# Splitting a bias on GpSimd instead of VectorE, and moving the statistics of the third batch ahead of the first sum of x1, in a one-core conv, MLP and mixture-of-experts block

## The reference

```python
h  = spiral_conv(ln(ln(x)) * gamma + beta)      # a complex decaying filter along the 1024 tokens
x1 = h + ln(x)
h  = ln(x1) * gamma + beta
x2 = x + silu(h @ w1 + b1) @ w2 + b2 + x1       # the dense layer; b2 is its second bias
out = x2 + experts(ln(x2))                      # 8 experts, the top two of each token
```

## Time and profile before

| | us |
|---|---|
| median of 3 runs (lowest, highest) | 457.8 (455.8, 460.84) |
| the profiled execution | 456.46 |
| its span, first to last instruction | 454.7 |
| PE busy | 374.8 |
| DVE busy | 345.9 |
| ACT busy | 320.1 |
| POOL busy | 274.8 |

### The profile page before, as it was taken

How to read it: one execution, slowest core, us unless ns; L and a number is a source line. 1 busy time by engine, 2 the same in 40 slices (tenths; PEclk the granted TensorE clock), 3 DMA queues, 4 the chain that set the end, 5 groups by cost and what they waited for, 6 DMA issues and landing times.

```text
span 454.7 us, 11189 instructions
## 1 busy us (share of the span) xinstructions
PE 374.8 (82%) x2716; PEld 322.2 (71%) x2716; DVE 345.9 (76%) x1310; ACT 320.1 (70%) x772; POOL 274.8 (60%) x339
## 2 busy tenths in 40 slices
PE   1273388797989797998994598999999999999970
PEld 1131257484858576776773498999999999999970
DVE  7999997978989988987628158777777777777770
ACT  5791586979797897977662565777777777777740
POOL 6990954575777798685747405775545454545451
PEclk9995599999989699999998579999999999999995
DMA  7649131020222222322212323454333333333200
GB/s 257 183 145 314 63 59 35 1 47 12 61 75 59 88 47 74 73 86 61 99 50 87 108 71 100 134 151 121 107 96 101 98 102 104 106 105 104 76 3 0
DMA packets 34434, 41.60 MB, mean 91 GB/s; under 512 B 5382, under 2 KB 29459, under 8 KB 34244
## 3 DMA queue, kind: packets, MB, share of 16 engines
q1 hardware_dynamic: 27236, 23.56, 18.1%
q0 software_dynamic: 7136, 17.33, 13.2%
HBM read 19.52 MB, written 18.92 MB: 85 GB/s over the span
## 4 chain that ended last, share of the span: by engine, by line
PE 59%; DVE 17%; issue 6%; POOL 5%; ACT 4%; POOLq 0%; DVEq 0%; ACTq 0%
PE up_p L998 12%; PE down_p L836 7%; PE up_p L825 7%; PE turn_p L998 6%; PE route_p L1017 6%; PE down_p L1017 6%; PE up_p L1017 6%; PE turn_p L813 5%; DVE stats L1097 3%; PE down_p L1007 2%; DVE work L1162 2%; DVE work L1160 2%; ACT work L648 2%; POOL sorted_rows L560 2%; PE route_p L874 2%
## 5 line engine op out<-in xcount | busy, mean ns | idle before, releaser
L597 POOL DMA_INDIRECT out<-result,out_id x91 | 89.2, 980 | 90.3 <-DVE result L1479 71.4
L560 POOL DMA_INDIRECT sorted_rows<-rows,pos x64 | 73.8, 1153 | 32.8 <-issue 16.8
L825 PE MATMUL up_p<-h_t,work 128*128 128x512 f32 x128 | 65.1, 638 | 10.4 <-ACT work L622 9.2
L836 PEld LDWEIGHTS down_p<-w_sb,work 128*128 128x128 f32 x512 | 60.6, 192 | 9.6 <-issue 9.6
L998 PE MATMUL up_p<-xt,work 128*128 128x128 f32 x488 | 66.5, 281 | 0.0
L787 ACT ACTIVATE work<-mw_c 128x256 f32 x182 | 65.6, 414 | 0.3 <-issue 0.2
L836 PE MATMUL down_p<-w_sb,work 128*128 128x128 f32 x512 | 63.0, 277 | 0.0
L998 PEld LDWEIGHTS up_p<-xt,work 128*128 128x128 f32 x488 | 61.0, 197 | 0.1
L772 ACT ACTIVATE hid_t<-up_p 128x512 f32<-128x512 f32 x61 | 36.4, 597 | 30.6 <-PE up_p L998 30.5
L813 PE MATMUL turn_p<-ident,work 128*128 128x128 f32 x192 | 29.7, 306 | 31.1 <-ACT work L648 11.5
L813 PEld LDWEIGHTS turn_p<-ident,work 128*128 128x128 f32 x192 | 25.2, 159 | 38.6 <-ACT work L648 11.6
(11 more groups left out here) (236 smaller groups left out, 810.2 us busy)
## 6 DMA issues: line engine op xcount, KB each, us to landing
tin<-sorted_rows SPq DMA_DIRECT2D x91, 136.0 KB, 2.1
resid<-in_x SPq DMA_DIRECT2D x8, 512.0 KB, 3.7
resid<-work POOLq DMA_DIRECT2D x8, 512.0 KB, 4.6
sorted_rows<-zeros SPq DMA_DIRECT2D x29, 136.0 KB, 2.2
out<-result,out_id POOLq DMA_INDIRECT x91
work<-in_mw SPq DMA_DIRECT2D x1, 1024.0 KB, 6.4
sorted_rows<-rows,pos POOLq DMA_INDIRECT x64, 2.5
work<-in_w SPq DMA_DIRECT2D x1, 256.0 KB
```

The lines of the kernel that those rows point to most:

```text
L560: g.indirect_dma_start(sorted_dram, bass.IndirectOffsetOnAxis(pos[b % 2][:, j:j + 1], 0), rows[b % ROWBUFS][:, j, :], None).then_inc(s_sor ...
L597: g.indirect_dma_start(out_rows, bass.IndirectOffsetOnAxis(out_id[k][:, :], 0), result[k][:, :], None, bounds_check=TOKENS - 1, oob_is_err ...
L825: t.matmul(dst, w1_g[:, k], half(h_t, h), start=True, stop=True).then_inc(s_up, 1)
L836: last = t.matmul(down_p[:, j * D:(j + 1) * D], silu[c % 2][:, j * TILE:(j + 1) * TILE], w2_sb[:, c, :], start=False, stop=c == FC - 1, sk ...
```

## The change

GpSimd now computes the remainder of the bias, in a new function `bias_halves` behind `sort_constants`, as three instructions, each awaited by the next; VectorE's two instructions for it are gone. And on VectorE the statistics and moments of x of batch 2 now stand ahead of `x1_sum(0)` and its statistics, where they stood behind them.

```diff
+            def bias_halves():
+                pool.wait_ge(s_whi, 1)
+                pool.wait_ge(s_ident, 1)
+                link(g.tensor_tensor(b2_lo, b2_rows, b2_hi[:, :].bitcast(f32), ALU.subtract))
+                link(g.tensor_scalar(b2_lo, b2_lo, ident[0:2, 1:2], None, ALU.mult))
+                g.tensor_tensor(b2_hi_lo[:, :], b2_lo, b2_first, ALU.add).then_inc(s_wsplit, 1)
...
             sort_constants()
+            bias_halves()
             x1_scales(0)
...
             def weights():
-                v.wait_ge(s_whi, 1)
-                link(d.tensor_tensor(b2_lo, b2_rows, b2_hi[:, :].bitcast(f32), ALU.subtract))
-                d.scalar_tensor_tensor(out=b2_hi_lo[:, :], in0=b2_lo, scalar=ident[0:2, 1:2], in1=b2_first,
-                                       op0=ALU.mult, op1=ALU.add).then_inc(s_wsplit, 1)
                 v.wait_ge(s_b1raw, 1)
...
             weights()
+            x_moments(2, x_statistics(2))
             x1_sum(0)
-            x_moments(2, x_statistics(2))
             rotated = rotate_re(1)
```

## The result

The changed kernel takes 464.9 us (median of 6 runs, 462.83 to 468.47), the kernel before 457.17 beside it (6 runs, 455.8 to 461.71). The ratio is 1.0154, 95% interval 1.009 to 1.0219: slower by about 7 us.

What follows compares the result with a forecast made beforehand. A prologue chain of waits through TensorE, VectorE, GpSimd and ScalarE was taken to bound the kernel. 0.2 + 3.5 + 2.0 - 0.1 = 5.6 us longer gave a forecast of 462.8 us, range 459.0 to 466.0.

Steps and rivals of the forecast that it cites:

- The lost cover: x1_scales(0) on GpSimd, no longer beside batch 2's one-operand statistics, waits on rotations and scans: 3.5 us longer.
- the four ends that the prediction names: x1_scales(0)'s instructions get through as rotate_re, rotate_im and two scans end: 46.3, 47.4, by 51.3 (power), 52.0.
- The bias: Three GpSimd instructions on 512 elements hold up batch 0's second scan, multiplies and subtraction on VectorE: 2.0 us longer.
- the upper end: Bias sized by GpSimd's own time: 1.3 us for each sum, 0.4 for the other instruction, 3.0 together.
- the row behind that term: Behind a 128-element GpSimd instruction begun at 23.29, a VectorE instruction took 1.31 for 1.21: 0.10 us, scaled to 512 elements.
- The 0.2: Batch 2's statistics on VectorE beside TensorE's turn end at 41.52, where x1_sum(0) began at 41.34: 0.2 us later.
- The 0.1: ScalarE's wait for x0_scales(2) between the norms at 54.54 and 57.82 goes: 0.1 us less.
- The cheap bias: Rival: GpSimd reads the bias between VectorE's instructions without holding them up; 3.6 us longer, 460.7; chance 0.20.
- The holder to its end: Rival: whichever engine came first holds the ports to its end, GpSimd's power included; 8.0 us longer, 465.1; chance 0.12.
- slip through: Not-slower rival: x1_scales(0) gets into gaps between VectorE's rotations and scans; 456.2 with a cheap bias; chance 0.07.
- slack behind the prologue: Rival: a later stage waiting on something else absorbs part, leaving 1 to 3 us; chance 0.11 with a shared gap.
- the port theory: GpSimd instructions reading SBUF and VectorE instructions with two SBUF operands exclude each other, each waiting for the other's reading.

Runs made afterwards that it cites:

- wait_as_cover: The changed kernel with VectorE waiting for the end of x1_scales(0) ahead of rotate_re(1); ratio to the kernel before 1.0116.
- cover_batch3: The changed kernel with the statistics of batch 3 moved from behind convolution(1) to directly behind x1_sum(0); ratio to the kernel before 1.0101.
- bias_late: The changed kernel with the bias on GpSimd moved behind add_x1(0), its rows in other buffers; ratio to the kernel before 1.012.
- reordered: The changed kernel with bias behind add_x1(0), x0_scales(2) ahead of x1_scales(0), and VectorE waiting for x1_scales(0) ahead of rotate_re(1); ratio to the kernel before 1.0133.
- bias_only: The changed kernel with the statistics of batch 2 put back behind x1_sum(0), so only the bias moves; ratio to the kernel before 1.0116.
- both_mended: The changed kernel with the diffs of cover_batch3 and bias_late together; ratio to the kernel before 1.0045.
- second_wait: both_mended with VectorE waiting for x1_scales(1) ahead of rotate_re(2); ratio to the kernel before 1.0004.
- before_waits: The kernel before with VectorE waiting for x1_scales(0) ahead of rotate_re(1) and x1_scales(1) ahead of rotate_re(2); ratio to the kernel before 1.0006.
- stats_only: The kernel before with only the statistics of batch 2 moved ahead of x1_sum(0), the bias left on VectorE; ratio to the kernel before 1.0129.

## Why the prediction was right

The places that the prediction names came out close to it: `x1_norm(0)` at 54.49 for 54.1, the first silu at 66.80 for 66.5, with 5.31 us of idle VectorE ahead of `x1_sum(1)`. The terms, one by one:

*The lost cover.* Forecast 3.5, measured 6.83 - 3.32 = 3.5. The four instructions got through at the four ends that the prediction names, one at each. wait_as_cover and cover_batch3 show that what matters is what VectorE does in that stretch: beside an idle VectorE the four took 2.4 us, beside one-operand statistics 3.3 (of which the last, already beside `rotate_re(1)`, took 1.16), beside rotations and scans 6.8.

*The bias.* Forecast 0.8 + 0.4 + 0.8 = 2.0, measured 3.44 - 2.35 = 1.1 in the scan, 0.4 and 1.0 in the multiplies, 2.5 in all. The mechanism was right and the two sums of two operands were sized too small: 512 elements cost VectorE some 1.0 to 1.1 each. That is about halfway between the 0.8 that I had taken and the 1.3 of the upper end. The estimate of 1.1 from the Trainium skill's figure for two operands (GPSIMD Engine Reference, 3.1) agrees with the 1.1 and 1.0 here; the sum itself lasts 1.26 on GpSimd (bias_late). The one-operand instruction cost the 0.4 forecast here, but 0.25 in reordered, and the row behind that term was thin. In the kernel before, the next GpSimd instruction on 128 elements waited for the end of the VectorE instruction of that row, at 24.66, and the one that VectorE ran behind it shows no loss. So the 0.4 owes something to luck:

```profile
23.65 1.16 POOL L505 CAST strict_b<-strict 128x128 bf16<-128x128 f32 x1
24.69 1.22 DVE L1367 TENSOR_TENSOR work<-work 128x1024 f32<-128x1024 f32 x1
```

The first of the three met the scan, at whose start it arrived 0.03 late and still got in, and not the multiply; since all are on the path that made no difference.

*The 0.2* for the statistics beside the turn was 2.7 - 2.5 = 0.2. The 0.1 that `x0_scales(2)` had cost ScalarE went: the norm at 63.73 follows without a gap.

*The rivals.* The cheap bias fell with bias_only, where the bias alone cost 2.5. The holder to its end fell with the power at 49.94: it ran until 53.52, and the second scan beside it, from 52.10, took its usual 2.35. That is the rule of the Trainium skill (SBUF — State Buffer, "SBUF: two separate sides") for GpSimd as the holder; here VectorE wasn't held while the power ran. `x1_scales(0)` didn't slip through. No slack behind the prologue took the loss back: the first silu was 5.9 late, the end 6.4.

*What the sum left out.* The forecast was 462.8 and the median 464.9. Against the kernel before, 5.6 us were forecast; the profiled runs differ by 6.4, the ratio makes about 7, the medians differ by 7.7. Of the excess, 0.3 arose in the prologue, by the bias. The rest lies behind the prologue and in runs that weren't profiled, of which the prediction says nothing. That its range took this in as well was luck. The profiled run of the changed kernel was the fastest of its six. The medians of all nine other runs, too, lie above what was expected, by 0.4 to 6.5 us.

TensorE's clock has a part in this. The stretch in which the profiled run of both_mended lost most, in windows, first of the kernel before, then of both_mended (columns: PE, PEld, DVE, ACT, POOL busy; granted clock as a share of 2.4 GHz, DMA share, GB/s):

```profile
61.50:83.00 21.50, 17.95 (x106) 12.99 (x106) 18.38 (x52) 15.84 (x34) 9.72 (x10) 1.00 0.15 29
84.50:94.80 10.30, 10.30 (x63) 7.62 (x62) 10.22 (x36) 10.04 (x23) 9.99 (x10) 1.00 0.27 52
...
61.50:83.00 21.50, 18.22 (x106) 12.90 (x106) 17.52 (x48) 14.52 (x31) 14.28 (x12) 1.00 0.17 32
84.50:94.80 10.30, 9.58 (x30) 6.95 (x31) 8.94 (x49) 6.79 (x14) 8.76 (x13) 0.50 0.27 52
```

From 84.5 to 94.8 the granted clock is at 1.2 GHz, where the profiled run before had 2.4; ScalarE was 1.5 us late as that stretch began and 6.0 behind it. TensorE had been busy for 18.22 of 21.5 us ahead of it, against 17.95 in the run before the change, which kept its clock, and 17.97 in second_wait, whose clock fell too (0.53 from 83 to 94). So busy time there doesn't tell them apart. Of the 12 runs of both_mended six had a mean clock of 0.924 or more and took 456.72 to 458.36; six had 0.918 or less and took 460.13 to 462.42. Runs with 0.918 or less are rarer in the kernel before (4 of 23 in the last comparison, at 460.9 to 461.61), but before_waits, where `x1_norm(1)` is only 0.15 late, had them in 6 of 12, and second_wait in 4 of 12.

Whether the changed kernel's last 1 to 2 us in the median, and the 2 or so of bias_only beyond its share, come from this isn't shown. The slowest run of the changed kernel has its lowest clock (468.47 at 0.908), but its fastest isn't the one with the highest (462.83 at 0.918; two at 0.922 took 464.14 and 464.5), and its profile has full clock from 83 to 94. What makes the clock fall more often stays open as well; no run here was made for it.

## What to carry to other kernels

An instruction on an idle engine isn't free if a busy engine has to wait while it reads: the bias cost GpSimd nothing and VectorE's critical scan and multiplies 2.5 us, while VectorE had done it at no cost in a wait. Before work is moved forward into a wait, ask what it was shielding where it stood: the 2.24 us of one-operand statistics let GpSimd's small steps run in 3.3 us, and without them they took 6.8. Where a short chain on GpSimd is on the path, one-operand work or even a wait on VectorE beside it can be better than work on two SBUF operands that nobody waits for: with the wait, the first silu came 4.2 earlier than in the changed kernel, of which `x1_norm(1)` kept 1.6. No version here was faster than the kernel before.

## What the runs showed that I had not expected

Whether a GpSimd instruction gets in at the end of a VectorE instruction can hang on a few hundredths of a us. The last one of `x1_scales(1)` took 0.50 to 0.51 when it began 0.44 us (before) or 0.46 (bias_only) ahead of the end of `rotate_re(2)`, and 0.56 to 0.92 when it began 0.51 to 0.86 ahead (changed, reordered, cover_batch3). It took 1.61 to 1.62 when it began 0.43 (stats_only, wait_as_cover), 0.42 (bias_late) or 0.41 (both_mended) ahead, having waited through `rotate_im(2)` too. A shift of 0.01 to 0.03 us made 1.1 us. Being early isn't all of it: two instructions that began 0.03 us behind the start of the next scan still got in, at 51.74 in the kernel before and at 33.30 in the changed one, both right behind a GpSimd instruction. Why, no run here shows.

VectorE's loss isn't GpSimd's own time: the one-operand instruction on 512 elements lasts 1.57 us undisturbed and cost VectorE 0.25 to 0.44, the two-operand ones last 1.26 and cost 0.97 to 1.09. And a power on 8 elements ran on for 1.45 us beside a scan that took its usual 2.35. That fits the port theory if GpSimd reads in only a part of such an instruction's time; no run here measured that part.
